# Two convolutions with group norm: group statistics through device memory instead of TensorE products

## The reference, cut to what matters

```
x: (16, 32, 128, 128) float32
def _gn(v, G=16, eps=1e-05):          # 16 groups of 2 channels
    m = mean(g, axis=(2, 3, 4)); s = var(g, axis=(2, 3, 4))
    return (g - m) / sqrt(s + eps)
w_masked = L0_conv_weight * mask       # mask from sum |weight| against a threshold
x = x + conv3x3(_gn(x), w_masked)
x = x + conv5x5(_gn(x), L1_conv_kernel) + bias
```

## Time and profile before

| | us |
|---|---|
| median of 3 runs (lowest, highest) | 948.56 (943.79, 949.09) |
| the profiled execution, its own time | 946.91 |
| its span, first to last instruction | 945.1 |
| TensorE busy | 825.8 (87%) |
| VectorE busy | 640.7 (68%) |
| ScalarE busy | 327.2 (35%) |
| GpSimd busy | 326.2 (35%) |

### The profile page before, as it was taken

How to read it: one execution, slowest core, us unless ns; L and a number is a source line. 1 busy time by engine, 2 the same in 40 slices (tenths; PEclk the granted TensorE clock), 3 DMA queues, 4 the chain that set the end, 5 groups by cost and what they waited for, 6 DMA issues and landing times.

```text
span 945.1 us, 108701 instructions
## 1 busy us (share of the span) xinstructions
PE 825.8 (87%) x52374; PEld 696.4 (74%) x52374; DVE 640.7 (68%) x998; ACT 327.2 (35%) x417; POOL 326.2 (35%) x146
## 2 busy tenths in 40 slices
PE   0154387999999999999999999999999999998884
PEld 0143265888888888888888888888888888887663
DVE  1757554777887788878787777778787877754210
ACT  0111222444433344334433344443334433432221
POOL 0200003333333444444444433333344444443322
PEclk9977597999999999999999999999999999999997
DMA  8967835988888888888889998888988767646322
GB/s 157 213 159 187 198 83 117 235 222 218 223 196 245 202 228 212 222 220 222 216 225 226 237 233 222 218 211 228 210 235 204 179 175 180 175 120 156 94 55 51
DMA packets 76413, 179.76 MB, mean 190 GB/s; under 512 B 18912, under 2 KB 19040, under 8 KB 68192
## 3 DMA queue, kind: packets, MB, share of 16 engines
q1 hardware_dynamic: 76384, 179.45, 77.5%
HBM read 112.30 MB, written 67.11 MB: 190 GB/s over the span
## 4 chain that ended last, share of the span: by engine, by line
PE 84%; issue 2%; ACTq 1%; POOL 0%; ACT 0%; POOLq 0%; DVE 0%
PE psum L578 82%; PE psum L643 1%; PE psum L637 1%; ACTq L337 1%; POOL mid L276 0%; ACT s L316 0%; POOLq L54 0%; ACT conv_out L307 0%; DVE gvar L454 0%; ACTq L306 0%; DVE bn_in L430 0%
## 5 line engine op out<-in xcount | busy, mean ns | idle before, releaser
L276 POOL TENSOR_TENSOR mid<-mid,conv_out 128x512 f32<-128x512 f32 x128 | 317.6, 2516 | 584.2 <-ACT conv_out L307 584.2
L578 PE MATMUL psum<-x_hi,s 32*32 32x512 f16 x25600 | 377.8, 380 | 16.3 <-ACTq L337 8.8
L578 PEld LDWEIGHTS psum<-x_hi,s 32*32 32x32 f16 x25600 | 336.0, 88 | 49.2 <-issue 14.2
L578 PE MATMUL psum<-x,s 32*32 32x512 f16 x13824 | 230.7, 397 | 25.0 <-DVE x L487 8.3
L578 PEld LDWEIGHTS psum<-x,s 32*32 32x32 f16 x13824 | 178.6, 88 | 75.4 <-issue 49.7
L578 PE MATMUL psum<-x_lo,s_hi 32*32 32x512 f16 x12800 | 212.6, 380 | 5.7 <-issue 5.0
L578 PEld LDWEIGHTS psum<-x_lo,s_hi 32*32 32x32 f16 x12800 | 159.9, 88 | 35.0 <-issue 16.4
L487 DVE TENSOR_TENSOR x<-x_bands,x 128x2304 f16<-128x2304 f32 x32 | 95.5, 2985 | 70.8 <-PE psum L578 70.8
L495 DVE TENSOR_TENSOR x_lo<-mid_bands,x_hi 128x2560 f16<-128x2560 f32 x32 | 90.4, 2826 | 53.6 <-PE psum L578 51.9
L307 ACT ACTIVATE conv_out<-psum,bias,unscale 128x512 f32<-128x512 f32 x128 | 94.3, 768 | 73.9 <-PE psum L578 73.9
L509 DVE SCALAR_TENSOR_TENSOR mid<-psum,unscale,x_own 128x512 f32<-128x512 f32 x128 | 89.8, 721 | 12.8 <-PE psum L578 12.4
(11 more groups left out here) (66 smaller groups left out, 165.0 us busy)
## 6 DMA issues: line engine op xcount, KB each, us to landing
x_own<-x_dram SPq DMA_DIRECT2D x128, 256.0 KB, 8.1
mid_scratch<-mid SPq DMA_DIRECT2D x128, 256.0 KB, 9.7
out_dram<-mid SPq DMA_DIRECT2D x128, 256.0 KB, 4.1
mid_bands<-mid_scratch SPq DMA_DIRECT2D x96, 320.0 KB, 7.6
x_bands<-x_dram SPq DMA_DIRECT2D x96, 288.0 KB, 5.5
mid_bands<-mid_scratch SPq DMA_DIRECT2D x32, 288.0 KB, 6.6
x_bands<-x_dram SPq DMA_DIRECT2D x32, 272.0 KB, 5.6
w<-L_conv_kernel_dram SPq DMA_DIRECT2D x4, 100.0 KB, 4.8
```

The lines of the kernel that those rows point to most:

```text
L276: nc.gpsimd.tensor_tensor(m, m, conv_out[:, b, :], ALU.add).then_inc(out_added, 1)
L578: ins = nc.tensor.matmul(psum[quad(j), bank + i, :].rearrange("p (a w) -> p a w", a=A), w[quad(i), at, :], src[quad(i), A * j + dy:A * (j ...
```

## The change

- TensorE no longer mixes statistics in the loop. VectorE's `bn_aggr` writes `mv`; ScalarE stores it (128 x 2 floats) in `mv_scratch` in device memory (`spread_stats`), waits until it has landed, and loads it back to all partitions (`gather_stats`, 128 partitions x 1 KB). VectorE then forms the group's mean and variance on its own with four 128x128 operations against `mix` (`group_stats`). Only the very first statistics still use two TensorE products, in `X5_BANK`.
- The four evictions of the 3x3 stand together, `bank3_go` is given right behind them, and the statistics of `mid` follow (`stats_out`).
- Scaling for the next step moves: `group_stats(s - 1)` stands between `low5` and `low3` of step `s`, `scale_of` behind `low3`.
- ScalarE: `spread_stats(s)` ahead of `high5`, `gather_stats(s)` behind it, `take_root` now behind `weights3` of the next step. In the lead both transfers stand behind `weights3` of the next step.
- The lead: weights arrive in the layout of taps (`w3`, `w5` as taps x output channels; the host turns the arrays), the 5x5 weights are waited for only after the first normalization, statistics of later tiles are taken later, `mid` of steps 0 and 1 is stored in two parts each, and both halves of `mid_bands` 0 and 1 are loaded together.
- TensorE's loop: a branch less between the two visits of `inner5`, and the semaphore and register instructions of a block are spread over taps (`inner5` at taps 10 and 14, `low_image` at 6 to 16). `keep_warm` puts eight 128x128 products ahead of the first 3x3. The tail is steered by adding 8 (`ALONE`) to the visit counter.

```diff
+            def spread_stats(s):
+                act.wait_ge(mv_ready, stat_number(s) + 1)
+                act.dma_start(mv_dram[s], mv[:, s % 2, :]).then_inc(mv_out, 16)
+            def gather_stats(s):
+                act.wait_ge(mv_out, 16 * (stat_number(s) + 1))
+                act.dma_start(every_mv[:, s % 2, :, :].rearrange("p q k -> p (q k)"),
+                              mv_dram[s:s + 1].rearrange("a q k -> a (q k)").to_broadcast([P, 2 * P]),
+                              ).then_inc(mv_in[s % 2], 16)
...
+                if 1 <= s <= 2:
+                    spread_stats(s - 1)
+                    gather_stats(s - 1)
+                if mixed_at(s - 1):
+                    take_root(stat_number(s))
...
+            def group_stats(s):
+                at = 0 if mixed_at(s)[0] == "x" else 1
+                dve.wait_ge(mv_in[s % 2], 16 * (s // 2 + 1))
+                means, variances = every_mv[:, s % 2, :, 0], every_mv[:, s % 2, :, 1]
+                nc.vector.scalar_tensor_tensor(product[:, 0, :], variances, 1.0, mix[:, :], ALU.mult, ALU.mult,
+                                               accum_out=sums[:, 0:1])
+                stat_step(nc.vector.scalar_tensor_tensor(product[:, 1, :], means, 1.0, mix[:, :], ALU.mult, ALU.mult,
+                                                         accum_out=gmean[:, at:at + 1]))
+                stat_step(nc.vector.scalar_tensor_tensor(deviation[:, :], means, gmean[:, at:at + 1], mix[:, :],
+                                                         ALU.subtract, ALU.mult))
+                stat_step(nc.vector.scalar_tensor_tensor(product[:, 0, :], deviation[:, :], float(Q * GROUP), deviation[:, :],
+                                                         ALU.mult, ALU.mult, accum_out=sums[:, 1:2]))
+                nc.vector.scalar_tensor_tensor(gvar[:, :], sums[:, 0:1], EPS, sums[:, 1:2], ALU.add, ALU.add).then_inc(var_ready, 1)
...
-                    if b:
-                        stats_mid(h, b - 1)
-                stats_mid(h, BANKS - 1)
+                dve.drain().then_inc(bank3_go, 1)
...
+            low3(0)
+            normalize_ahead(0)
+            take_conv3(0)
+            stats_in(3, range(BANKS))
+            aggregate("x", 1, 0, mv_ready)
+            stats_out(0)
+            low3(1)
+            group_stats(0)
+            scale_of("x", 1)
+            normalize_ahead(1)
+            take_conv3(1)
...
-                    if t == 6:
-                        mix_mean()
-                    if t == 15:
-                        mix_var()
...
-                pe.br_lt(step, HALVES, on_true="more3", on_false="no3")
-            with nc.body("more3", valid_engines=only):
-                pe.br_lt(visit5, 2, on_true="inner3", on_false="last5")
+                pe.br_lt(visit5, 2, on_true="inner3", on_false="no3")
+            with nc.body("no3", valid_engines=only):
+                pe.br_eq(visit5, ALONE + 1, on_true="inner5", on_false="last5")
```

More of the change, by code:

```diff
@@ L170, in mixed_at, with stat_number @@
             return None
+        def stat_number(s):
+            return sum(1 for t in range(s) if mixed_at(t))
         def quad(q):
@@ L544, in _ @@
                     clear_pad(1, s + 1 - LAG, scalings)
+            setup3()
+            stats_in(0, range(BANKS))
+            stats_in(1, range(BANKS))
+            aggregate("x", 0, 1, mean_go)
+            first_mean()
+            first_variance()
+            scale_of("x", 0)
+            dve.wait_ge(zeroed, 7)
+            scalings = 0
+            normalize_ahead(-1)
+            dve.drain().then_inc(bank3_go, 1)
+            dve.wait_ge(w_loaded, 16 * 2 * Q)
+            largest(w5, 1)
@@ new lines, in _ @@
+            stats_out(1)
+            aggregate("mid", 0, 1, mv_ready)
+            stats_in(4, range(BANKS))
+            stats_in(5, range(BANKS))
+            for s in range(2, STEPS):
+                if s > HALVES:
+                    dve.drain().then_inc(bank3_go, 1)
+                if has5(s):
+                    low5(s - LAG)
+                if mixed_at(s - 1):
+                    group_stats(s - 1)
+                if has3(s):
+                    low3(s)
+                if mixed_at(s - 1):
+                    scale_of(mixed_at(s - 1)[0], stat_number(s))
+                normalize_ahead(s)
@@ L545, in _ @@
                 if has3(s):
                     take_conv3(s)
[L547 to L565 removed]
+                    stat = mixed_at(s)
```

235 lines of the change are left out of this document (113 added, 122 removed).

## The result

The changed kernel takes 1087.26 us (median of 4 runs, 1079.92 to 1090.34), the one before 946.31 on the same chip (943.79 to 949.09): ratio 1.148, 95% interval 1.140 to 1.156. The prediction was 883 us with a range to 912. The profiled execution took 1084.25 us.

A forecast was written before the change was run, and what follows sets the result against it. TensorE's own stream was taken to bound the steady steps, waits the lead and tail. 946.9 - 42 (stream) - 17.6 (lead) - 4 (tail) = 883.3, forecast 883 us, range 868 to 912.

The forecast's parts named there:

- What must hide for that: Steady steps: the statistics' store, load and VectorE operations were to fit into idle time without stalling TensorE.
- L1: Landing time of ScalarE's statistics store, taken as 3.2 us.
- L2: Landing time of ScalarE's statistics load (128 KB), taken as 4.0 us.
- The ring's formula: Statistics' path over two steps: 15.6 + 13.1 + 0.2 + 2(L1 + L2) against 47.4; slower than TensorE only over 9.2.
- the third rival: Small stores among bulk packets take 6.5 and 6.0 us, steps 27.0 us, 986 us in all; chance 8%.
- TensorE's stream, -42: Steady steps 4 to 31: products and pauses removed save 1.5 us a step, 28 x 1.5 = 42 us.
- Group statistics on VectorE, 1.45 us in VectorE's pause: Between low5 and low3: four 128x128 operations at 0.30 us each, 1.45 us in all, fit in 1.77 us idle.
- ScalarE's allowance for the store, 4.7 us: Steady steps: every us of the store's landing beyond 4.7 stalls TensorE; at 3.2 there is none.
- The lead, -17.6: Before the steady steps: first 3x3 -16.4, step 0 -5.0, steps 1 and 2 +2.4 each, first full step -1.0.
- The two accounts: What the change takes out of TensorE's stream, times 28, and what it does to the waits of the lead.
- The first rival: Steady steps: transfers become the limit, a step is 24.2 us or more, 897 to 910 us; chance 16%.

The follow-up runs named there:

- e2: The changed kernel with both small transfers issued by GpSimd instead of ScalarE: 1056.21 us.
- e9: The changed kernel with band loads of x and mid after the first two halves cut to one row, and their scaling turned into a clamp: 981.79 us.
- e10: The changed kernel plus one wait: in x's steps SyncE holds mid's band loads and what follows until the statistics store has landed: 979.38 us, ratio 1.037.
- e12: e1 with the 1 KB statistics store issued by ScalarE, waited for by nobody until VectorE's next statistics 20 us later: 948.00 us.
- e16: e15 plus e10's wait on SyncE: 946.13 us, ratio 1.000.
- e15: The changed kernel with both transfers and waits, but storing 512 bytes of each partition instead of 8, statistics from a constant tile: 1017.19 us.
- e11: The changed kernel with more held: x's band loads also wait for the store, and in mid's steps mid is stored first: 1025.11 us.
- e5: e1 with GpSimd's adds of the 5x5 cut from 512 columns to one: 869.58 us.
- e8: The kernel before with the changed start, the fourth x tile's statistics later and the change's TensorE loop, group products kept: 914.31 us, ratio 0.966.
- e1: The changed kernel without its two small transfers, group_stats reading a constant tile: 891.77 us, ratio 0.945.
- e6: The changed kernel with only the store kept and waited for by ScalarE, no load, group_stats on a constant tile: 1012.78 us.
- e4: The kernel before with the changed start alone, statistics staying on TensorE: 938.53 us, ratio 0.993.
- e14: e12 with the store moving 512 bytes of every partition, 128 packets of 512 bytes: 894.92 us, ratio 0.945.
- e13: e12 with the store moving one partition's two numbers, one packet of 8 bytes: 895.31 us, ratio 0.943.

## Why the prediction was wrong

**The step that failed** is in "What must hide for that": "ScalarE's transfers have no such queue ahead of them, so I take values near the low end: L1 = 3.2, L2 = 4.0". Measured from issue to the point where the waiting engine can go on: L1 = 11.85 in x steps and 7.21 in mid steps, 9.5 on average, L2 = 6.9. The sum is 16.4 instead of 7.2. The bounds in the rows were right (3.1, 9.7, 11.9); the choice between them was wrong, because it took a queue for a matter of who issues. e2, e9 and e10 show in its place that a small transfer waits for what any engine issued ahead. The lead shows it for the load: in step 2 it is issued at 78.62, in the middle of eight loads of bands of mid that SyncE began at 75.36, and takes 14 us. A second part could be read in no row of before: packets of 8 bytes signal 1.0 to 2.6 us later than those of 512 and hold up TensorE (e12 to e16).

**The ring's formula held.** It is 14.45 us, half of 15.6 + 13.1 + 0.2, plus L1 + L2. With both taken as the mean of x steps and mid steps (the load up to its landing) it gives 31.0 for the changed kernel (30.64 measured), 27.0 for e10 (26.92), 25.6 for e16 (25.82) and 29.4 for e15 (28.49), where the loads of mid's steps take 9.6 us and those of x's 6.8. Two lie off the other way: e9, 25.9 against 27.21, which has the pauses, and e11, 25.0 against 28.53, which has the new wait. So the third rival had mechanism, place and threshold: "It decides from L1 + L2 = 10.7". It was given 8%, and its landings of 6.5 and 6.0 were too short as well: 986 us, 101 under the measured time.

**TensorE's stream, -42.** This part was right. e5, where nothing else is late, has steps of 23.57 us against 23.7 predicted, 1.65 less than before; e8 gives 0.53 of it by the loop alone, where I counted 0.55.

**Group statistics on VectorE, 1.45 us in VectorE's pause.** Mis-sized where GpSimd adds at the same time: the line between 0.16 and 0.72 us gives 0.30, which e5 confirms (0.29 to 0.38); e1 has 1.17 to 1.27 each. This is worth 22 us (e1 against e5). In the changed kernel GpSimd mostly stood idle by then.

**ScalarE's allowance for the store, 4.7 us.** The mechanism was right, the size conservative: in e6 a store of 11.9 us stopped TensorE for 5.2, so 6.7 were hidden. It is not a part of the ring but a cost beside it: the store alone costs 121 us (e6), 56 of them without any wait (e12), which leaves 65 for ScalarE's wait and the clock behind it. In steady steps: e1 24.23 us, e12 26.53, e6 28.36, the changed kernel 30.64. The prediction had nothing for the second of these, since it took the store to cost only what is waited for.

**The lead, -17.6.** First 3x3 at 26.92 (28.0 predicted), step 0 16.5 us (14.8), step 1 24.5 (21.6), step 2 35.9 (25.9): the first eviction of step 4 comes at 164.56 instead of 167.4, 2.8 us early and not 17.6. The waits named were the right ones, VectorE's for `every_mv` in steps 1 and 2, but they last 8.82 and 17.28 us where some 7 had been expected. For late tiles the prediction allowed up to 2 us, for the second one, and nothing for tiles 2 and 3 (e4). In its step 1 the terms 0.5 + 3.2 + 0.5 + 4.0 make 8.2, not the 7.7 that it adds, a slip of half a microsecond in each of steps 1 and 2.

**The sum.** Steps: 27 x (30.64 - 23.7) = 187; lead 15; together 202, and the profiled execution lies 1084.25 - 883.3 = 201 above the forecast. The two accounts close. The first rival, transfers as the limit at 24.2 us a step, didn't appear: e5 runs steps of 23.57 us with all large transfers.

**Open.** Why packets of 8 bytes hold up TensorE's stream, 15 us after the store too, no trace here shows; only that 128 of them do and one, or 128 of 512 bytes, don't. e2's store, recorded as 16 packets of 64 bytes, has 22 such pauses. Code that is loaded late is no likely reason: none of the 13 transfers of code that e12's trace records between 150 and 750 us falls into one of its 24 pauses. Where between 8 and 512 bytes it ends wasn't tried. A form of the statistics in device memory with large packets that computes everything wasn't built either. I estimate it at e16's 946 us or more, as long as the order of transfers stays; the products on TensorE (e8, 914 us) beat that.

## What to carry to other kernels

A round trip through device memory in a loop costs what was issued ahead of it, whoever issued it: look in the timeline at what the bulk queue issues in the 5 us before, and price the trip by that queue's median or worse, not by its fastest transfer. Where such a trip is needed, hold the bulk issuer back by one wait on the step with slack, and only there. Make the packets hundreds of bytes long (512 was the one size tried), and before paying for any of it see what the removed instructions cost by themselves: here 1.1 us a step against a trip of 16.

## What the runs showed of the hardware

- 31 stores of 128 packets of 8 bytes, waited for by nobody, cost 56 us (948.0 against 891.8, e12 and e1; 51 by the ratios); 128 packets of 512 bytes (e14) or one of 8 (e13) cost nothing clear of noise.
- Packets of a second issuer started 6.2 us after their issue with 2.4 MB issued in the 5 us ahead (changed kernel, x steps), and 1.1 us after it with mid's 1.28 MB of them held back (e10).
- A 128x128 VectorE operation with two inputs takes 0.32 us alone (e5) and 1.27 beside GpSimd's adds (e1).
- After a stop of 5.2 us TensorE ran at 0.50 of its clock over the 3.8 us looked at, and 144 matmuls took 4.07 us instead of 2.35 (e6): a stop costs more than its length.
